# Routing and weight loads of the last mixture of experts, moved into the causal attention jobs

## The reference, cut to what matters

```python
x = x + tanh(g_xattn[0]) * cross_attention(ctx, layernorm(x), b, seq_len)      # unit 0, masked
x = x + tanh(g_ffn[0])   * attention_plus_small_moe(layernorm(x))              # unit 1, top 2 of 8
x = x + tanh(g_xattn[1]) * attention_with_extra_keys(layernorm(x), ctx)        # unit 2
x = x + tanh(g_ffn[1])   * causal_block(layernorm(x))                          # unit 3

def causal_block(x):                         # 16 heads of width 16, F = 1024, E = 8, K = 2
    q, k, v = split(x @ w_qkv)
    attn = softmax(where(causal, q @ k.T / sqrt(hd), lowest))
    h = layernorm(x + (attn @ v) @ w_o, g1, b1)
    probs = softmax(h @ wg)
    topv, topi = top_k(probs, K);  topv = topv / topv.sum(-1)
    w = sum(topv * one_hot(topi, E))
    h1 = gelu(einsum('bsd,edf->ebsf', h, w1) + bb1)
    y = einsum('ebsf,efd->ebsd', h1, w2) + bb2
    return layernorm(h + einsum('ebsd,bse->bsd', y, w), g2, b2)
```

## Time and profile before

| what | value |
| --- | --- |
| median of 3 runs | 2578.48 us |
| runs, lowest to highest | 2577.73 to 2580.44 us |
| the profiled execution | 2577.39 us |
| its span on the core | 2575.0 us |
| its mean granted TensorE clock | 0.943 of full speed |
| causal jobs, from the first gate copy to the last | 1578.5 to 1884.6 us |
| from the last gate copy to the first expert matmul (L1846) | 1884.7 to 1964.9 us |
| expert tiles | 1964.9 to about 2482 us |

### The profile page before, as it was taken

The page is one execution under the profiler, slowest core; times in us unless marked ns, Lnnn a source line. Parts: engine busy times, 40 slices in busy tenths (PEclk is TensorE's granted clock), DMA queues, the critical chain, the costliest instruction groups (busy, mean ns, idle before and its releaser), DMA issues. The chain is left out here.

```text
span 2575.0 us, 52660 instructions
## 1 busy us (share of the span) xinstructions
PE 2187.5 (85%) x17577; PEld 1565.6 (61%) x17578; DVE 1586.2 (62%) x4073; ACT 1388.9 (54%) x2454; POOL 1168.6 (45%) x2040
## 2 busy tenths in 40 slices
PE   1888886988889999989899999999837999999950
PEld 1454454655556655555566666766527999999950
DVE  3788777743444787776777777787554444443337
ACT  3688874544546777776677788777601222222212
POOL 5555423566655553332332347887601333333323
PEclk9999997999999999999999999999956999999985
DMA  6877826325456765555455445556273111111125
GB/s 185 217 190 183 186 76 151 91 89 153 115 155 161 184 179 122 132 129 130 109 134 126 114 110 118 138 123 139 53 231 134 33 36 36 36 35 34 35 84 196
DMA packets 225776, 314.22 MB, mean 122 GB/s; under 512 B 36011, under 2 KB 159911, under 8 KB 219306
## 3 DMA queue, kind: packets, MB, share of 16 engines
q1 hardware_dynamic: 205322, 263.37, 40.7%
q0 software_dynamic: 13728, 35.68, 4.6%
q10 hardware_dynamic: 6528, 12.58, 1.3%
HBM read 215.02 MB, written 98.33 MB: 122 GB/s over the span
## 5 line engine op out<-in xcount | busy, mean ns | idle before, releaser
L1178 ACT ACTIVATE ex<-t_ps 128x512 f32<-128x512 f32 (+1 forms) x1280 | 685.6, 579 | 206.4 <-PE t_ps L1084 152.8
L1494 DVE TENSOR_REDUCE mx<-s_ps 128x2 f32<-128x512 f32 (+1 forms) x1024 | 658.7, 684 | 196.3 <-PE s_ps L1055 114.6
L1084 PE MATMUL t_ps<-qs,ks 123*128 123x256 bf16 x2048 | 363.7, 281 | 28.9 <-ACT ex L1178 14.9
L1107 PE MATMUL pv_ps<-ex,va 128*17 128x256 f32 (+1 forms) x5120 | 324.4, 381 | 1.1 <-POOL ex L1248 0.5
L1846 PEld LDWEIGHTS x_up_ps<-x_rows_t,x_wnow 128*128 128x128 f32 x2272 | 267.3, 193 | 5.3 <-issue 0.9
L1084 PEld LDWEIGHTS t_ps<-qs,ks 123*128 123x128 bf16 x2048 | 174.1, 100 | 157.8 <-ACT ex L1178 75.6
L1846 PE MATMUL x_up_ps<-x_rows_t,x_wnow 128*128 128x128 f32 x2272 | 267.9, 277 | 1.1 <-DVE x_pre L1909 0.7
L1172 ACT ACTIVATE qs<-tr_ps 27x2048 bf16<-27x2048 bf16 x128 | 239.5, 1871 | 52.7 <-PE tr_ps L1068 49.7
L1876 ACT ACTIVATE x_rows_t<-x_rt_ps 128x256 f32<-128x256 f32 x72 | 27.7, 385 | 442.1 <-PE x_rt_ps L1835 442.1
L1856 PE MATMUL x_y_ps<-wdn,x_act 128*128 x1136 | 257.1, 379 | 0.7 <-DVE x_y L1917 0.7
L1061 PE MATMUL s_ps<-ks,qs 99*128 99x256 bf16 (+1 forms) x1024 | 191.9, 290 | 59.9 <-DVE mx L1494 48.5
(11 more groups left out here) (317 smaller groups left out, 3994.0 us busy)
## 6 DMA issues: line engine op xcount, KB each, us to landing
q_parts<-pq SPq DMA_DIRECT2D x128, 192.0 KB
qs<-q_parts SPq DMA_DIRECT2D x64, 384.0 KB
qs<-q_parts SPq DMA_DIRECT2D x192, 128.0 KB
k_parts<-pk SPq DMA_DIRECT2D x96, 192.0 KB
ks<-k_parts SPq DMA_DIRECT2D x96, 192.0 KB
ks<-k_parts SPq DMA_DIRECT2D x288, 64.0 KB
ks<-ctx_k_parts SPq DMA_DIRECT2D x64, 192.0 KB
ks<-ctx_k_parts SPq DMA_DIRECT2D x192, 64.0 KB
```

The costliest lines, as they stand in the source:

```text
L1084: last = pe.matmul(dst[:, t * T:(t + 1) * T], key[0:ROWS, h, t * P:(t + 1) * P], qs[q_at][0:ROWS, h, :], start=True, stop=True)
L1107: last = pe.matmul(pv_ps[i * VS:i * VS + VW, q0:T], val[:, t, k * QH + i, :], e, start=r == 0 and t == 0, stop=r == srcs - 1 and t == NT - ...
L1178: act.activation(ex[:, n % EXPS, 0:w], t_ps[n % 2][:, 0:w], ACT.Exp).then_inc(t_read, 1)
L1494: dve.tensor_reduce(dst, s_ps[n % S_BANKS][:, :].rearrange("p (a b) -> p a b", a=dst.shape[-1]), AX.X, ALU.max).then_inc(s_read, 1)
```

## The change

1. `route` is gone. The softmax, the choice of experts and the slots are computed in unit 3, in four **picks**: after the gate logits of batches 4, 9, 13 and 15, for 5, 5, 4 and 2 batches. A pick is the steps PA, PX (exponential on ACT), PB (three), PC, PR (two matmuls and the sums on DVE), PQ; the running count of each expert goes from pick to pick. After the last one PT makes the tables `expert_of` and `room_of`.
2. Each expert has a fixed room of 4096 slots, so that a pair's slot is known as soon as its rank is. The names of pairs (4 bytes each) are scattered to a DRAM table `slot_names` (128 x 256) by 64 indirect DMAs on POOL, the steps PS, four in a job (8 behind the last pick). In setup one iota and one DMA of 128 KB fill the table with a name that is out of bounds.
3. The three instructions of QSPLIT in unit 3 go from POOL to DVE. The norm's scale and shift, HNG, stay on POOL.
4. `wup` and `wdn` now lie in one tensor `arena`, whose space the attention buffers `qs`, `ex`, `pq`, `pk`, `aq`, `ak`, `w0`, `wproj`, `w1x`, `xn`, `ctx`, `xt` and `ks` use first. SP issues the weight loads in the attention phase, as each part falls dead: LWA (3 MB, after unit 2), LWP (2.5 MB), LWX (1 MB), LWK (4 of 1 MB), LWQ (3 of 1 MB), LWE (2.5 MB, after the last PV). In SP's list LWA stands behind the stores of the query parts of batch 11 and ahead of the store of the key parts of batch 10 and the loads of the query and key rows of batches 10 and 11; the others stand behind the last batch's key rows, between the last stores.
5. `run_experts` gets a block in front: SP loads `bup` and `bdn`; POOL waits for all 64 scatters and loads the names; DVE makes `row_of` from them. In the loop POOL finds a tile's column by a `value_load` of `room_of`, once for the gather and once for the scatter. The loads of `c_h` and `c_x` for `combine` go from in front of the loop to after the fifth tile's result (`y_done` of 6). `c_y` lies in `arena`.
6. The planner gets costs for the new steps, and ranks PS and the weight loads last among steps of one job.

```diff
+    "PA": [("dve", 0.7)], "PX": [("act", 0.35)], "PB": [("dve", 1.4)], "PR": [("pe", 0.5), ("dve", 2.6)], "PQ": [("dve", 1.8)], "PC": [("dve", 0.8)], "PS": [("pool", 1.05)], "PT": [("dve", 5.0)],
...
+STAGES_OF_UNIT = {("QSPLIT", 3): [("dve", 1.65)], ...
+ROOM = B * T
+ROOMS = E * ROOM // P
+PICKS = {4: 5, 9: 5, 13: 4, 15: 2}
...
+        for k in range(TOPK * PICKS[b] * NT):
+            needs[("PS", u, scatter_job(b, k), (b, k))] = [r]
...
-    return 0 if op[0][0] in ("OT", "FIN", "M", "MT", "RC", "RX", "RANK", "RH", "TH", "NAME") else 1
+    return 0 if op[0][0] in (..., "PA", "PX", "PB", "PR", "PQ", "PT") else 2 if op[0][0] == "PS" or op[0][0][0:2] == "LW" else 1
...
+                    elif name == "LWA":
+                        wait_turned(sp, ("PROJ", 2, B - 1, 0))
+                        sp.wait_ge(vc_ready, max(VC_AT[("VC", 2, m, 0)] for m in range(B - NCTX, B)) + 1)
+                        for n in range(3):
+                            load_down(n)
...
+                    elif name == "PS":
+                        at, n = k
+                        pool.wait_ge(slots_picked, PICK_NTH[at] + 1)
+                        m, t = n % TOPK, (at + 1 - PICKS[at]) * NT + n // TOPK
+                        pool.indirect_dma_start(names_d.rearrange("p (r n) -> (p r) n", n=1), bass.IndirectOffsetOnAxis(ap=p_at[:, m, t:t + 1], axis=0),
+                                                p_names[:, m, t:t + 1], None).then_inc(names_stored, 16)
...
+                    elif name == "QSPLIT":
+                        wait_copied(dve, ("Q", u, b, 0))
...
+                        s.done(dve.tensor_tensor(rest[:, :, :], rest[:, :, :], parts[:, :, 0, :], ALU.subtract))
+                        s.wait()
+                        s.done(dve.tensor_copy(parts[:, :, 1, :], rest[:, :, :]))
+                        s.wait()
+                        dve.tensor_tensor(parts[:, :, 2, :], rest[:, :, :], parts[:, :, 1, :], ALU.subtract).then_inc(late_split, 1)
...
-            route(nc, e)
...
+            @block.gpsimd
+            def _(pool):
+                pool.wait_ge(a["names_stored"], 16 * TILES * TOPK)
+                pool.dma_start(names[:, 0:ROOMS], a["names_d"]).then_inc(names_loaded, 16)
...
                 def column(z, n):
-                    return z[:, n:n + 1] if isinstance(n, int) else z[:, bass.ds(n, 1)]
+                    at = slice(n, n + 1) if isinstance(n, int) else bass.ds(n, 1)
+                    return z[:, bass.ds(pool.value_load(room_of[0:1, at], min_val=0, max_val=ROOMS), 1)]
...
+                sp.wait_ge(y_done, 6)
...
+                pe.wait_ge(a["ew_loaded"], 16 * 3 * E)
                 turn(1, 1, 0)
```

More of the change, by code:

```diff
@@ L1383, in _ @@
                         wait_turned(dve, step)
-                    if name == "RC":
+                    if name in ("PA", "PB", "PR", "PQ", "PC", "PT"):
+                        s.wait()
+                        pick(name, step, b, bank_of(step) if name == "PR" else None)
+                    elif name == "RC":
                         if chain:
@@ L1754, in run_experts @@
         ps = lambda name: own.enter_context(nc.psum_tensor(name, [P, 512], F32))
-        ident, expert_of, row_of, dest_of, wup, wdn, bup, bdn = (a[n] for n in ("ident", "expert_of", "row_of", "dest_of", "wup", "wdn", "bup", "bdn"))
+        ident, expert_of, room_of, row_of, names, wup, wdn, bup, bdn = (a[n] for n in ("ident", "expert_of", "room_of", "row_of", "names", "wup", "wdn", "bup", "bdn"))
         HALF = F // 2
@@ L1822, in _ @@
                 pool.wait_ge(loaded[0], 16 * (LAST // 2 + 2))
+            @block.sync
+            def _(sp):
+                sp.wait_ge(y_done, 6)
+                for q in range(RING):
+                    sp.dma_start(flat_pair(a["c_h"][q]), a["hn_d"][2 * q:2 * q + 2].rearrange("b p t n -> p b (t n)")).then_inc(a["c_loaded"][q], 16)
+                    sp.dma_start(flat_pair(a["c_x"][q]), a["xb_d"][2 * q:2 * q + 2].rearrange("b p t n -> p b (t n)")).then_inc(a["c_loaded"][q], 16)
             @block.tensor
```

419 lines of the change are left out of this document (231 added, 188 removed).

## The result

The changed kernel takes 2620.61 us (median of 4 runs, 2614.28 to 2622.46), the kernel before, run beside it, 2579.46 us. The ratio is 1.0149, with a 95% interval of 1.0129 to 1.0169: the kernel is 1.5% slower, where 2557 us, a gain, was forecast, with a range of 2532 to 2597. The profiled execution has a span of 2618.7 us, 43.7 more than before.

The account below looks back on a forecast made before the run. PE was taken to bound the expert tiles and nearly fill the causal jobs, in a ring with DVE; a serial chain bounds the seam. 2577.4 - 48 (seam) + 25 (causal jobs) + 3 (experts) = 2557 us, range 2532 to 2597.

Parts of the forecast that it names:

- DVE in the causal jobs: Unit 3: splits and picks take DVE from 184 to 237 of 240 us; 12 us lost, bounds 0 and 35.
- Rival B: Causal jobs: DVE fills up, splits and picks wait behind POOL; 50 us lost instead of 25, about 2582; chance 0.10.
- SP and the wire: Causal jobs: LWA's 3 MB ahead of batch 10 and 11 rows, and batch 9's key split; 6 us lost, bounds 0 and 15.
- POOL: 7 us forecast: Causal jobs: 26 us more POOL work fits idle time except in the last jobs; 7 us lost, bounds 0 and 13.
- The seam: Last gate copy to first expert matmul: 80.2 us becomes 32, 48 saved; bounds of the seam 26 and 47 us.
- The expert tiles: Expert loop: tile period stays 7.24 us; c_h and c_x loads crossing gathers cost 3 us, bounds 0 and 10.
- Rival A: Expert loop: POOL's value loads do not run ahead, a tile takes 7.80 us; 40 us more, 2597; chance 0.17.
- port rule: DVE splits: VectorE and GpSimd share ports under an exclusive lock; every split would wait about one POOL operation twice.
- the 2.6 us of the forecast: Causal jobs: DVE time taken per split, 1.9 us when clean, more beside POOL's operations; 12 splits, 31 us.

Follow-up runs that it names:

- b3: Kernel before plus five unused 128 x 512 DVE additions behind each unit 3 gate copy: ratio 1.0300; 597.7 us from unit 2's eleventh result to last gate copy.
- b1: Kernel before with only unit 3's query splits moved to DVE, planned anew: 2561.8 us against 2548.3, one execution each.
- c3: Changed kernel, scatters unplanned and issued at end, LWA loaded last, splits on POOL: 542.3 us from unit 2's eleventh result to last gate copy.
- c1: Changed kernel with scatters kept out of the plan and issued at the end: 553.5 us from unit 2's eleventh result to last gate copy.
- c2: Changed kernel, scatters kept out of the plan and issued at the end, LWA loaded last: 563.9 us from unit 2's eleventh result to last gate copy.
- f1: The changed kernel itself again, in another set: ratio 1.0101 to the kernel before; 574.5 us from unit 2's eleventh result to last gate copy.
- g1: Kernel before with ACT's routing exponential issued ahead of its 16 weight loads: 2540.6 us against 2551.0, ratio 0.9956.
- b2: Kernel before plus eight unused POOL additions in one piece ahead of batch 6's second row-maxima turn in unit 3: ratio 1.0036 to the kernel before.
- b6: Kernel before plus eight POOL additions in one piece and 60 narrow PE transposes ahead of the resulting wait: ratio 1.0050 to the kernel before.
- f2: Changed kernel with LWA's 3 MB loaded at the end of SP's list: 2579.5 us against 2577.7 for the changed kernel in the same set.
- e1: Changed kernel, 64 scatters issued after the last scale, other order kept: 2630.7 us; 573.4 us from unit 2's eleventh result to last gate copy.
- b4: Kernel before plus eight unused POOL additions, one ahead of each row-maxima turn of batches 5 to 8 in unit 3: ratio 1.0025 to the kernel before.
- d1: Changed kernel; POOL waits for all scatters before ending the attention block, c_h and c_x loads wait for y_done of 60: seam 41.1 us.

## Why the prediction was wrong

**DVE in the causal jobs: the step that failed.** The forecast had DVE's added work about right: a split takes 0.79 + 0.43 + 0.69 = 1.9 us at the median and 2.35 in the mean of 16, against 2.6, and splits and picks add 57.7 us of DVE time in length A. What failed is the term that turned it into time: a stretch of 12 us, because DVE had 56 of 240 us free. The free time was not free to use. It is made of waits in a ring in which PE, DVE, ACT and POOL hand each head's scores on; work put in front of a row maximum delays the scores behind it, and this comes back to PE, as PE's waits in b3 show. b3 gives 76 to 81 us for 63 us of DVE time, of which some 12 are waits for POOL. Splits and picks measured one by one give 11 to 15 (b1, where POOL was relieved of 36 us) and 21 to 25 us (c3), together with the weights 36 to 47 (c1, c2), each by one execution. The upper bound of 35 us, "two thirds of the new work", was nearer than the centre of 12.

**Half of it is PE's own time, at a lower clock.** From the earlier trace rows I read a full PE at clock 1.00 and did not ask what happens to it when PE stalls. With 12 matmuls more, PE's busy time in length A went from 475.9 to 514.1 us and its idle time from 41 to 76: 38 us of the 73 are PE itself, slower (in f1 against g1, 24 of 53). By and large the clock of the table falls with the length, and b2 shows one stall and the slow matmuls behind it. How much of the length would be left if the clock stayed up is not shown, since b6 did not hold it up. Rival B had the nearest number for this stretch, 50 us, and a part of what happened, waits of DVE behind POOL; but DVE did not fill up (71% of length A), and it lacked the clock. That its loss was near is in part luck.

**SP and the wire: 6 us forecast, none found** (f2, without LWA in front, took 1.8 us more than f1 at the median).

**POOL: 7 us forecast, more found, with an open size.** Taking the scatters out of the plan brought length A from 575 to 590 down to 554 to 564, some 10 to 35 us; taking only their time away (e1) brought nothing that can be seen. This points at the order which the planner made to fit them, by single executions. The planner's own lengths point the same way: 504 before, 512, 515, 519, 534 and 557 stand in the same order as the measured 517, 532, 542, 554 to 564, 573 to 590 and 596, with about half the growth. They could have been read ahead of the forecast, as a list to rank by and not as times. I weighed 26 us of additional work against 18% of idle time, the same mistake as with DVE: b4 lost 3 to 10 us for 10 us of POOL time set apart. In the last two jobs, the only place where the forecast charged it, PE's waits for the norm's scale grew by 6 us, about as forecast.

**The seam: 48 us gained forecast, 40.4 measured.** Pick, scatters, names load and the gather are each within 1 us of the working. Two terms were too small: the end of the attention block, 9.2 us where 2.1 stood for the landing, and the end of the names' block, 2.7 us where 0.9 stood, because SP's issue of `bdn` lasts longer. In the trace of before the attention block ends on POOL with ordinary operations, and the expert loop's end has 2.8 us.

**The expert tiles: 3 us forecast, 9.5 measured.** Rival A, POOL as the bound with 7.80 us a tile, did not happen: the second value load lies beside the gather, as the run-ahead on DVE had suggested, and the period is 7.24. Of the 9.5 us 6.3 are `c_h` and `c_x` crossing the gathers, the mechanism of the forecast at twice its size, and some 3 are late gathers near the end (PE waits 2.06 us for one of them, 0.65 before), whose cause is open.

**The ports of DVE and POOL.** The port rule of the Trainium skill, "SBUF — State Buffer", section "SBUF: two separate sides", would have made a split wait for POOL's operations. The traces agree with that. The first operation of a split, with two SBUF inputs, has 681, 792 and 1691 ns as shortest, median and longest; seven of the 16 took over 1 us, and each of these began while POOL was in an addition, subtraction or cast of 128 x 512. This is the longest, which ends 0.55 us after POOL's:

```profile
1712.59 1.27 POOL L1376 TENSOR_TENSOR o<-o,wexp 128x512 f32<-128x512 f32 x1
1712.72 1.69 DVE L1702 TENSOR_TENSOR arena<-arena 128x512 f32<-128x512 f32 x1 [0.23 <-ACT arena L1297]
```

The last operation of a split happened to meet none of those (691, 693 and 774 ns). In sum it is some 9 us of DVE's time over the 16 splits, which the 2.6 us of the forecast had allowed for, and not the 50 us of rival B. In b3 the waiting is some 12 us of DVE's time and up to 18 us of POOL's. How much of the length came this way is not shown.

## What to carry to other kernels

Idle time of an engine inside a tight ring is not room: until a trace shows otherwise, count most of the work added to any engine of the ring as time (from a third to all of it here, and more in b3, with what PE loses at the lower clock). A chain that stands alone at a seam is cheap to shorten where it stands (one instruction ahead of 16 DMA issues gave 9 us of the seam here), and moving it into the full part is paid for there. A list scheduler that ranks new work last can still reorder the old work around it, so read its own times for the old steps before and after.

## What the runs showed of the hardware that I had not expected

- Ending the attention block on POOL behind the scatters takes 8.5 us (the DRAIN in d1) although all of them have landed and the DMAs are idle; the gap is 9.2 us in the changed kernel and 10.6 with the wait for the landing in it. Ending the expert loop, also behind indirect DMAs, took 2.8 us in the kernel before.
- The granted TensorE clock fell from 1.00 to 0.76 and 0.82 in the 16 us from a stall of 6.8 us on, and to 0.92 and 0.65 when narrow transposes filled half of that stall.
- An indirect DMA of 128 names of 4 bytes takes POOL 0.96 us and 0.30 to the next, about as much as one of 128 rows of 1 KB (1.00 and 0.30).
- An addition or subtraction of 128 x 512 on DVE with two SBUF inputs takes 0.68 us at its shortest and 1.53 to 1.69 at its longest, beside POOL's operations of 1.15 us or more (b3 and the changed kernel).
- POOL's value loads run ahead of its engine: the second of a tile adds 0.34 us in front of the copy.
